# Two turns of feed-forward weights converted a stage ahead, and the feed-forward turns grouped as 4, 4, 4 and 2 tiles instead of 2, 4, 4, 2 and 2

## The reference, cut to what matters

```python
# second block: cross attention over latents and context
q = (latents @ Wq.T); k = (hidden @ Wk.T); v = (hidden @ Wv.T)
out = softmax(q k^T / sqrt(96)) v
x = layernorm(x + out @ Wo.T)
# third block: feed-forward on weights stored as integers, groups of 128 rows
def dequantize(imatrix, scales, zeros, group_size, out_dtype):
    rs = jnp.repeat(scales, group_size, axis=0)
    rz = jnp.repeat(zeros, group_size, axis=0)
    return ((imatrix.astype(rs.dtype) - rz.astype(rs.dtype)) * rs).astype(out_dtype)
gate = silu(x @ gate_proj)      # 512 x 1792
up = x @ up_proj                # 512 x 1792
x = layernorm(x + (gate * up) @ down_proj)   # 1792 x 512
```

## Time and profile before

| | |
|---|---|
| median of three runs | 1649.45 us |
| the profiled execution | 1650.77 us |
| its span in the trace | 1649.0 us |
| mean granted TensorE clock | 0.983 of full |
| PE busy in the span | 94% |
| feed-forward stage, first weight matmul to the last row block | 529.17 to 733.97 us |

### The profile page before, as it was taken

One profiled execution on the slowest core, in us unless ns is written; L12 is line 12 of the kernel. 1 busy time (PEld: TensorE's weight loads), 2 busy tenths in 40 slices (PEclk: granted clock), 3 DMA queues, 4 the chain that ended last, 5 costly groups with the idle time before them and its releaser, 6 DMA issues. The chain is left out here.

```text
span 1649.0 us, 29540 instructions
## 1 busy us (share of the span) xinstructions
PE 1552.9 (94%) x10984; PEld 1290.7 (78%) x10984; DVE 951.0 (58%) x1693; ACT 798.9 (48%) x2426; POOL 768.0 (47%) x624
## 2 busy tenths in 40 slices
PE   6999999999998779998999889999999999999997
PEld 4777888888886557876777678888888888888875
DVE  3947503333356777778677835555555555555656
ACT  3342324444443445445988734454455445445532
POOL 3403215343321779763533527655455545554413
PEclk9999999999999899999999999999999999999999
DMA  6100200010101743204000021201101011010001
GB/s 211 39 1 1 58 20 21 21 38 5 53 1 46 230 134 128 90 1 122 1 2 27 27 91 39 65 26 39 35 31 52 17 49 39 27 33 14 1 1 51
DMA packets 61777, 77.84 MB, mean 47 GB/s; under 512 B 12168, under 2 KB 41348, under 8 KB 61636
## 3 DMA queue, kind: packets, MB, share of 16 engines
q1 hardware_dynamic: 61172, 74.63, 14.4%
q0 software_dynamic: 464, 1.32, 0.3%
HBM read 73.85 MB, written 2.10 MB: 46 GB/s over the span
## 5 line engine op out<-in xcount | busy, mean ns | idle before, releaser
L1152 POOL TENSOR_TENSOR xa_rs<-xa_ms,minus_half 128x5 f32<-128x5 f32 x64 | 74.8, 1168 | 160.5 <-DVE xa_ms L1423 160.3
L1158 POOL TENSOR_TENSOR xa_prob<-xa_prob,xa_inv 128x512 f32<-128x512 f32 x64 | 66.7, 1042 | 139.0 <-DVE xa_inv L1390 139.0
L766 POOL TENSOR_TENSOR xa_prob<-xa_prob,xa_inv 128x1024 f32<-128x1024 f32 x32 | 60.7, 1895 | 140.8 <-DVE xa_inv L1029 140.8
L1418 DVE TENSOR_REDUCE xa_ssq<-pre 128x4 f32<-128x512 f32 x64 | 43.9, 686 | 134.4 <-ACT pre L1354 134.4
L1368 ACT ACTIVATE xa_prob<-xa_prob,xa_peak 128x128 f32<-128x128 f32 x256 | 99.7, 391 | 41.9 <-DVE xa_peak L1434 41.9
L101 PE MATMUL late_bank<-late_q_hi,xT_hi 128*128 128x512 f32 x284 | 117.9, 415 | 0.0
L1745 DVE SCALAR_TENSOR_TENSOR ff_acc<-ff_ring,ff_sT,ff_acc 128x512 f32<-128x512 f32 x140 | 100.6, 747 | 21.1 <-ACT ff_acc L1699 14.5
L103 PE MATMUL late_bank<-late_q_lo,xT_hi 128*128 128x512 f32 x284 | 112.6, 397 | 0.0
L102 PE MATMUL late_bank<-late_q_hi,xT_lo 128*128 128x512 f32 x284 | 112.5, 396 | 0.0
L1354 ACT ACTIVATE pre<-late_bank 128x512 f32<-128x512 f32 x64 | 38.2, 597 | 141.3 <-PE late_bank L103 141.3
L1985 POOL TENSOR_TENSOR pre<-pre,sa_inv 128x1024 f32<-128x1024 f32 x32 | 63.7, 1989 | 92.0 <-DVE sa_inv L2192 92.0
(11 more groups left out here) (414 smaller groups left out, 4929.9 us busy)
## 6 DMA issues: line engine op xcount, KB each, us to landing
pre<-in_wq SPq DMA_DIRECT2D x8, 1024.0 KB, 5.7
late_raw_o<-in_wo SPq DMA_DIRECT2D x8, 1024.0 KB, 5.3
ff_dn_q<-in_down_w SPq DMA_DIRECT2D x7, 512.0 KB, 3.9
ff_dn_z<-in_down_z SPq DMA_DIRECT2D x7, 512.0 KB, 5.0
ff_dn_s<-in_down_s SPq DMA_DIRECT2D x7, 512.0 KB, 5.8
pre<-in_wq SPq DMA_DIRECT2D x16, 192.0 KB, 3.4
pre<-in_wo SPq DMA_DIRECT2D x16, 192.0 KB, 3.8
pre<-in_xT SPq DMA_DIRECT2D x4, 512.0 KB, 8.1
```

What stands on the lines that cost most here:

```text
L766: pool.tensor_tensor(prob[:, t % 3, :, :], prob[:, t % 3, :, :], bc(inv[:, t % 3, :], 2, [P, Q, KEYS]), ALU.mult).then_inc(s["norm"], 1)
L1152: pool.tensor_tensor(rs[:, :], ms[:, :], m.minus_half[:, 0:Q + 1], ALU.pow).then_inc(s["rs"], 1)
L1158: pool.tensor_tensor(prob[:, u % 2, :, :], prob[:, u % 2, :, :], bc(inv[:, u % 2, :], 2, [P, Q, S]), ALU.mult).then_inc(s["norm"], 1)
```

## The change

Turns 0 and 1 are loaded and converted during the cross-attention stage, on DVE, after the work of steps 24, 25 (turn 0) and 28, 29 (turn 1), into two buffers that both stages share. SP of that stage loads turns 0, 1 and 2 into `m.pre`, each when the one before is converted. In the feed-forward stage turns are grouped (0,1), (2,3), (4,5), (6,); there are 8 half blocks instead of 10 and 32 row blocks instead of 40. The units of the weight pieces and of the down weights, and the places of the row blocks, are rewritten, and SP's list has the gate and up weights behind the down weights of each turn.

```diff
+    WEIGHTS_AT = ((24, 24, 25, 25), (28, 28, 29, 29))
...
-                ffn_stage_inputs(sp, io, *ffn_stage_buffer(m.pre), 0, s["ld_next"])
-                sp.wait_ge(s["ld_next"], 96)
+                for T in range(3):
+                    if T:
+                        sp.wait_ge(s["w"], KC * T)
+                    ffn_stage_inputs(sp, io, *ffn_stage_buffer(m.pre), T, s["ld_w"])
+                sp.wait_ge(s["ld_next"], 32)
+                sp.wait_ge(s["ld_w"], 64 * 3)
...
+                def weights(T, c):
+                    q, z = ffn_stage_buffer(m.pre)
+                    if c == 0:
+                        dve.wait_ge(s["ld_w"], 64 * (T + 1))
+                        if T == 0:
+                            dve.wait_ge(s["q_mm"], 3 * B)
+                        else:
+                            dve.wait_ge(s["rows"], 3 * B)
+                    dve.tensor_tensor(ffn_weights(m.early.w[T])[:, c, :, :], q[:, c, :, :], z[:, c, :, :], ALU.subtract).then_inc(s["w"], 1)
...
-GROUPS = ((0,), (1, 2), (3, 4), (5,), (6,))
+GROUPS = ((0, 1), (2, 3), (4, 5), (6,))
...
-        mid = {3: [0, 1], 4: [2, 3], 5: [4, 5], 6: [6], 7: [7], **{n: [n - 1] for n in range(9, 22)}, 22: [22], 23: [24, 25], 24: [26, 27],
-               25: [28, 29], 26: [30, 31], 27: [32, 33]}
-        end = {21: [21], 22: [23], 27: [34, 35]}
+        mid = {**{n: [n - 5] for n in range(5, 25)}, 25: [20, 21], 26: [22, 23], 27: [24, 25]}
+        end = {27: [26, 27]}
...
-        weight_units = {1: (1, 2, 2, 2), 2: (4, 4, 5, 5), 3: (7, 8, 9, 10), 4: (10, 11, 12, 13), 5: (14, 15, 16, 17), 6: (18, 19, 20, 21)}
-        down_units = {0: (1, 1, 1, 2, 2, 2), 1: (3, 3, 4, 5, 5, 6), 2: (6, 6, 7, 7, 7, 8), 3: (10, 10, 11, 12, 12, 13),
-                      4: (14, 14, 15, 16, 16, 16), 5: (18, 18, 19, 20, 20, 21), 6: (22, 22, 23, 24, 24, 25)}
+        weight_units = {2: (4, 5, 5, 6), 3: (7, 8, 8, 9), 4: (10, 11, 12, 13), 5: (14, 15, 16, 17), 6: (18, 19, 20, 21)}
+        down_units = {0: (1, 1, 1, 2, 2, 2), 1: (3, 3, 3, 4, 4, 4), 2: (6, 6, 7, 8, 8, 8), 3: (9, 9, 10, 11, 11, 12),
+                      4: (13, 13, 14, 15, 15, 16), 5: (17, 17, 18, 18, 19, 19), 6: (21, 21, 22, 23, 23, 24)}
...
                 for T in range(TURNS):
-                    if 0 < T < TURNS - 1:
-                        if T >= 2:
-                            sp.wait_ge(s["w"], KC * (T - 1))
-                        else:
-                            sp.wait_ge(s["w_first"], KC)
-                        ffn_stage_inputs(sp, io, *stage[(T + 1) % 2], T + 1, s["ld_even" if T % 2 else "ld_odd"])
                     if T:
                         sp.wait_ge(s["dn_sub"], T)
                         sp.wait_ge(s["dn_w"], MT * T)
...
                     sp.dma_start(dn_s[:, :, :], io["down_s"][part, :].partition_broadcast(P)).then_inc(s["ld_dn"], 16)
-                    if T == 0:
-                        ffn_stage_inputs(sp, io, *stage[1], 1, s["ld_odd"])
-                sp.wait_ge(s["w"], KC * LAST)
+                    if T + 3 < TURNS:
+                        if T:
+                            sp.wait_ge(s["w"], KC * T)
+                        ffn_stage_inputs(sp, io, *stage[(T + 3) % 2], T + 3, s["ld_even" if T % 2 else "ld_odd"])
+                sp.wait_ge(s["w"], KC * (LAST - 1))
...
-                    if n and hb % 2 == 0 and k % MT == 0:
-                        pe.wait_ge(s["w"], KC * turn_of(n))
+                    if turn_of(n) >= 2 and hb % 2 == 0 and k % MT == 0:
+                        pe.wait_ge(s["w"], KC * (turn_of(n) - 1))
                     for i in range(4):
-                        if n == 0:
-                            pe.wait_ge(s["w_first"], i + 1)
                         group(n, i)
...
-                        dve.wait_ge(s["ld_odd" if T % 2 else "ld_even"], 64 * ((T + 1) // 2))
                         if T >= 3:
+                            dve.wait_ge(s["ld_odd" if T % 2 else "ld_even"], 64 * ((T - 1) // 2))
                             dve.wait_ge(s["grp"], last_use(T - 3))
...
-                q, z = stage[0]
-                for c in range(KC):
-                    dve.tensor_tensor(w[:, 0, c, :, :], q[:, c, :, :], z[:, c, :, :], ALU.subtract).then_inc(s["w_first"], 1)
```

More of the change, by code:

```diff
@@ L52, in __init__ @@
         self.norm_bank = None
+class Early:
+    def __init__(self, sb):
+        self.w = [sb(f"early_w{n}", [P, KC * 2 * WIDE], F32R) for n in range(2)]
 class Late:
@@ L649, in cross0_stage, with pieces @@
         SLOT = KC * FEATS
+        def pieces(flat):
+            return [flat[:, n:n + FEATS] for n in range(0, flat.shape[1], FEATS)]
         raw_k, raw_v = (m.pre[:, n * SLOT:(n + 1) * SLOT].rearrange("p (c n) -> p c n", c=KC) for n in range(2))
@@ L652, in cross0_stage @@
         raw_o = m.pre[:, SLOT:2 * SLOT].rearrange("p (j n) -> p j n", j=BLOCKS)
-        wide_hi, wide_lo = (sb(n, [P, 2, SLOT], F32R) for n in ("wide_hi", "wide_lo"))
-        k_hi, k_lo, v_hi, v_lo = (w[:, n, :].rearrange("p (c n) -> p c n", c=KC) for n in range(2) for w in (wide_hi, wide_lo))
-        q0_hi, q0_lo = (sb(n, [P, SLOT], F32R) for n in ("q_hi", "q_lo"))
+        wide_hi = [sb("wide_hi", [P, SLOT], F32R)[:, :], m.early.w[1][:, 0:SLOT]]
+        wide_lo = [sb(f"wide_lo{n}", [P, SLOT], F32R)[:, :] for n in range(2)]
+        v_hi, v_lo = (w[1].rearrange("p (c n) -> p c n", c=KC) for w in (wide_hi, wide_lo))
+        k_hi, k_lo = (pieces(w[0]) for w in (wide_hi, wide_lo))
+        q_rest = sb("q_lo", [P, SLOT - FEATS], F32R)
+        q0 = pieces(m.early.w[0][:, 0:SLOT + FEATS]) + pieces(q_rest)
         spare_hi, spare_lo = (x[:, 0:3, :].rearrange("p c n -> p (c n)") for x in (m.cT_hi, m.cT_lo))
@@ L669, in cross0_stage @@
         s = {n: sem("xa0_" + n) for n in (
-            "k_hi", "k_lo", "v_hi", "v_lo", "ld_q", "ld_o", "ld_next", "hi", "split_q", "split_o", "pre_mm", "pre_ev", "q_mm", "q",
+            "k_hi", "k_lo", "v_hi", "v_lo", "ld_q", "ld_o", "ld_next", "ld_w", "w", "hi", "split_q", "split_o", "pre_mm", "pre_ev", "q_mm", "q",
             "score", "peak", "exp", "inv", "norm", "turn", "prT", "pv", "out_hi", "out_lo", "rows", "add")}
@@ L675, in wq @@
         def wq(i):
-            hi, lo = (q0_hi, q0_lo) if i % 2 == 0 else (spare_hi, spare_lo)
-            return [w[:, 0:SLOT].rearrange("p (c n) -> p c n", c=KC) for w in (hi, lo)]
+            return (q0[0:KC], q0[KC:2 * KC]) if i % 2 == 0 else [pieces(w[:, 0:SLOT]) for w in (spare_hi, spare_lo)]
         def wo(i):
-            return [w[:, 1 - i % 2, :].rearrange("p (j n) -> p j n", j=BLOCKS) for w in (wide_hi, wide_lo)]
+            return [w[1 - i % 2].rearrange("p (j n) -> p j n", j=BLOCKS) for w in (wide_hi, wide_lo)]
         def mixed(w, c):
@@ L688, in blocks @@
         def blocks(w, c):
-            return w[:, c, :].rearrange("p (j g f) -> p j g f", g=G, j=BLOCKS)
+            return w[c].rearrange("p (j g f) -> p j g f", g=G, j=BLOCKS)
         def block(w, c, j):
-            return w[:, c, j * P:(j + 1) * P]
+            return w[c][:, j * P:(j + 1) * P]
         def wide_blocks(f):
@@ L1038, in _ @@
                         batch_scale(dve, m, n1, u % B)
+                    for T in range(2):
+                        for c in range(KC):
+                            if WEIGHTS_AT[T][c] == t:
+                                weights(T, c)
 def cross1_stage(nc, m, io, sem):
@@ L1474, in ffn_stage_buffer, with ffn_weights @@
     return [flat[:, n * KC * 2 * WIDE:(n + 1) * KC * 2 * WIDE].bitcast(INT32).rearrange("p (c a n) -> p c a n", c=KC, a=2) for n in range(2)]
+def ffn_weights(flat):
+    return flat[:, :].rearrange("p (c a n) -> p c a n", c=KC, a=2)
 def ffn_scales(sp, io, dest, done):
@@ L1504, in ffn0_stage @@
         stage = [ffn_stage_buffer(m.pre), ffn_stage_buffer(other)]
-        w = sb("w", [P, 3, KC, 2, WIDE], F32R)
+        w = [ffn_weights(x) for x in (*m.early.w, sb("w", [P, KC * 2 * WIDE], F32R))]
         sT = sb("sT", [P, 2, KC, TILES])
@@ L1644, in group @@
                     bank = ring[q % RING]
-                    pe.matmul(bank[:, :], w[:, T % 3, c, a, f], m.xT_hi[:, c, cols], start=True, stop=False)
-                    pe.matmul(bank[:, :], w[:, T % 3, c, a, f], m.xT_lo[:, c, cols], start=False, stop=True).then_inc(s["grp"], 1)
+                    pe.matmul(bank[:, :], w[T % 3][:, c, a, f], m.xT_hi[:, c, cols], start=True, stop=False)
+                    pe.matmul(bank[:, :], w[T % 3][:, c, a, f], m.xT_lo[:, c, cols], start=False, stop=True).then_inc(s["grp"], 1)
                 def out_rows(r):
@@ L1777, in _ @@
                     part(n, 3)
-                    for T in range(1, TURNS):
+                    for T in range(2, TURNS):
                         for c in range(KC):
@@ L2358 @@
 SHARED = 4
+PAIRED = (1, 2)
 def program(nc, io):
@@ L2368, in program @@
         m.scales, m.own = sb("scales", [P, P]), sb("own", [P, HC])
+        pair = ExitStack()
         for n, stage in enumerate(STAGES):
             used = []
```

(4 more changed lines are left out.)

4 lines of the change are left out of this document (2 added, 2 removed).

## The result

The changed kernel takes 1684.16 us in the median of four runs (1680.5 to 1688.2), against 1649.12 for the kernel before in four runs: a ratio of 1.0209, interval 1.0193 to 1.0225, slower by 35 us. The forecast was 1681.9, with a range of 1664 to 1693. The profiled execution took 1685.62 us, with a span of 1683.8.

What follows compares the result with a forecast made beforehand. PE was taken as the bound, busy 94% of the span, with 27.5 us lost in the feed-forward stage. Loss after 16.6 + 42.1 + 0.7 = 59.4, +31.9, plus 0.5 in cross attention: 1681.9 us, range 1664 to 1693.

Steps and rivals of the forecast that it cites:

- Part 3: SP's new list: DVE waits for down loads in units 6, 9 and 13; 14.0 us each, 42.1 in all.
- the 1.75: Extra us for PE's slow restart after a gap, read from nine slow matmuls at 545.65 to 549.50 us.
- Part 2: Feed-forward front, units 0 to 5: POOL's list delays row block 0; 14.9 us plus 1.75 restart, 16.6 lost.
- POOL's 20 operations: Products, totals, lows and down-weight work before row block 0, at 1.40 us each, ending at 564.6 us.
- The rival in which DVE paces: Feed-forward front: DVE, not POOL, sets the pace; 5 us lost, not 16.6; 1670 us; chance 0.08.
- Part 1: Converting turns 0 and 1 in cross attention costs +0.5 us, bounds 0 and 3.0.
- Part 4: The rest: same 760 matmuls, DVE's dropped row additions gain 0, two small waits in the back cost 0.7 us.
- The sum: Feed-forward loss 27.5 us before, 59.4 after, +31.9; with cross attention's +0.5, +32.4.
- loads that land independently: Rival at the stalls: down loads land beside the four before them, 8.3 us, not 13.5; 1666 us; chance 0.08.
- The third, no stalls: Rival: down loads come early enough, so the front's gain of 9.7 us stands alone; 1640 us; chance 0.04.

Runs made afterwards that it cites:

- e10: The kernel of e1, with POOL scaling only 32 of 512 columns of the down weights of turns 0 and 1; 1637.4 us.
- c0: The changed kernel run again without any edit, on the chip of the next three runs; 1682.9 us.
- e2: The changed kernel, with SP issuing the three down loads first after the same wait and the four gate and up loads behind them; 1664.95 us.
- e1: The changed kernel, with SP's down loads of each turn from 2 on placed before the wait for that turn's conversion; 1640.57 us.
- e4: The changed kernel, with 34 idle products of PE before pair 3 of units 7, 10 and 14; 1683.4 us.
- e3: The changed kernel, with the down-weight steps of turns 2, 3 and 4 one unit later (7, 10, 14); 1663.4 us.

## Why the prediction was right

By its own steps:

- *Part 3, the three stalls,* is confirmed by name, place and size. Forecast: loads 13.5 us behind the last piece, PE idle for 12.3, restart 1.75, 42.1 for the three. Measured: waits of 13.1, 13.1 and 12.8 us, gaps of 11.6, 12.3 and 11.3, restarts of 2.7 on average, 43.2 in sum. The loads were a little faster and the restart was dearer by 0.95, with 12 to 15 slow matmuls where eight were forecast. The two errors cancel in part. Why the restart is dearer is not shown: the stalls are longer than the 5.7 us gap of the earlier trace rows on which the 1.75 stood, but a wait of 2.1 us before row block 0 is followed by 2.6 as well. The four loads of the earlier trace rows took 8.9 us, not 9.0, which changes nothing here.
- *Part 2, the front:* 16.6 us forecast, of which 14.9 up to row block 0; measured 562.92 - 528.30 - 20.5 = 14.1, and 2.6 for the restart, 16.7. That the sums agree so well is luck: the list ended 0.8 us earlier than forecast and the restart was dearer by 0.9. The mechanism held: POOL's 20 operations run from 535.51 to 562.87 us, 1.37 us each, with hardly an idle moment; row block 0 was released by POOL, and e10 shows the pacing. What the prediction did not name is how the loss arises. Only 2.1 of the 14.1 us is the wait for POOL at row block 0. Three waits before it (2.1, 1.1 and 2.5 us) are for banks that ACT frees late, because ACT's queue stands for 2.3 to 3.6 us each time on a product of POOL, and 6.4 us are matmuls that start further apart than 0.23 us. The rival in which DVE paces falls.
- *Part 1, cross attention:* +0.5 forecast, 0.02 measured. The stretch of 94.20 us is the same within 0.03 in nine profiles with and without the pieces. The lower bound was the right one: measured from the first load of turn 0, the maximum of step 29 starts 1.1 us later than before, and the next instruction of DVE at the same time as before, since its wait for ACT shrinks from 1.32 to 0.21 us.
- *Part 4:* 0.7 forecast for the back; what remains is 61.3 - 16.7 - 43.2 = 1.4.
- *The sum:* +31.9 for the stage, measured 61.3 - 27.5 = +33.8, and +32.0 in c0's profile. The rest of the 35 us is within what executions differ by: the same program behind this stage took 916.9 us in this profile, 913.5 in the one of c0 and 915.0 in that of the kernel before.
- *The rivals:* loads that land independently are ruled out by the waits of 13 us, where that rival had 8.3, and by e2; a front paced by DVE by e10. The third, no stalls, was priced at 1640 us; that is what e1 measures, 1640.6, with the list in the other order.

## What to carry to other kernels

A queue written as one list makes each entry wait for all the waits in front of it: when a load is moved, read who stands behind its wait and in which unit that one is needed, not only when the moved load is needed itself. Here a prefetch with time to spare stood ahead of a load that had none, and it cost a change that was otherwise worth 8.6 us another 43.6. And PE's six banks let it run on for about 4 us behind a late engine (3.9 by the prediction's count; at the first stall PE stops at 578.31, 4.05 us after DVE began to wait); what goes beyond is paid in full, with a slow restart on top.

## What the runs showed of the hardware

TensorE's restart: after gaps of 11 to 12 us the next 12 to 15 matmuls cost 2.5 to 2.9 us more, at a granted clock of 0.50 (590 to 595.5 us). The length of the last gap alone does not decide it: row block 0 of the changed kernel comes after a wait of 2.10 us and runs at 0.50 (563 to 568 us), the one of e10 comes after 2.03 us and runs at 1.00 (561.4 to 566 us). And in e4 five matmuls after a gap of 3.8 us ran at full rate before the granted clock fell to its lower level (0.63 us shown for one, in place of 0.39), so the slow ones are not always the first.

POOL beside DVE: in the changed kernel's front a total of POOL takes 2.19 us where others take 1.26 (1.26 to 1.30 for most of its operations there), and begins 0.16 us behind a `down` of DVE:

```profile
536.78 1.22 DVE L1784 TENSOR_TENSOR ff_dn_w<-ff_dn_q,ff_dn_z 128x1024 f32<-128x1024 int32 x1
```

```profile
536.94 2.19 POOL L1632 TENSOR_TENSOR ff_acc<-ff_acc 128x512 f32<-128x512 f32 x1
```

DVE ends at 538.00, and 538.00 + 1.26 = 539.26 against POOL's end at 539.13, as if POOL waited until DVE had finished and then ran at its own length. It goes the other way round too: in e3 a `down` of DVE starts at 551.63, 0.27 us behind a product of POOL, and takes 4.59 us in place of 1.22. Three operations of POOL stand one behind the other until 555.14, and 555.14 + 1.22 = 556.36 against DVE's end at 556.22. No run tried such a pair by itself. These times agree with the rule of the Trainium skill's page SBUF — State Buffer, section Who interferes with whom, that a VectorE operation with two inputs in SBUF and a GpSimd operation that reads SBUF contend for one port pair, which is held exclusively.
